# Score differences placed between a tile's two score pairs, half as many of them beside experts, and one list of steps for all units

## What is computed

```python
# attention of layers 0, 1 and 3 (biases and norms left out)
scores = jnp.einsum('bhqd,bhkd->bhqk', q, k) / jnp.sqrt(jnp.float32(8))   # 16 heads, 1024 x 6404
attn = jax.nn.softmax(scores, axis=-1)            # layer 2: jax.nn.sigmoid(scores)
ctx = jnp.einsum('bhqk,bhkd->bhqd', attn, v)
x = x + ctx @ Wo.T
# experts, layer 0 (layers 1 and 3 also gated, layer 1 run twice; layer 2: gelu, not gated)
h = silu(a) * g                                   # a, g = halves of x @ c_fc[e]
x = x + sum over the two chosen experts of weight * (h @ c_proj[e])
```

## Time and profile before

| | |
|---|---|
| median of 3 runs | 4747.94 us (4747.63 to 4750.8) |
| profiled execution, its own time | 4733.75 us |
| its span, first to last instruction | 4731.8 us |
| mean granted TensorE clock | 0.953 |
| busy: PE / DVE / ACT / POOL | 84% / 59% / 84% / 18% |
| busy in us: DVE / ACT | 2803.3 / 3983.6 |

### The profile page before, as it was taken

The page is one execution under the profiler, slowest core; times in us unless marked ns, Lnnn a source line. Parts: engine busy times, 40 slices in busy tenths (PEclk is TensorE's granted clock), DMA queues, the critical chain, the costliest instruction groups (busy, mean ns, idle before and its releaser), DMA issues. The chain is left out here.

```text
span 4731.8 us, 68983 instructions
## 1 busy us (share of the span) xinstructions
PE 3965.9 (84%) x26742; PEld 911.7 (19%) x26742; DVE 2803.3 (59%) x5598; ACT 3983.6 (84%) x4403; POOL 829.8 (18%) x719
## 2 busy tenths in 40 slices
PE   3578888888888888888898999888888888888887
PEld 2112111111112221122112222111111111122112
DVE  1487888778877778877610111011287568886833
ACT  2478998889978898888899888978998888888994
POOL 3001000340014410143522011012001120035002
PEclk7579999999989999999999999999999999999998
DMA  2212000110002110011102121100001100011001
GB/s 73 84 42 56 20 13 18 31 29 10 13 26 56 30 47 10 19 47 35 37 13 61 37 74 40 35 31 26 13 13 36 32 13 13 14 32 32 10 1 47
DMA packets 105922, 150.33 MB, mean 32 GB/s; under 512 B 23064, under 2 KB 64032, under 8 KB 105584
## 3 DMA queue, kind: packets, MB, share of 16 engines
q1 hardware_dynamic: 105584, 145.82, 10.9%
HBM read 122.24 MB, written 23.51 MB: 31 GB/s over the span
## 5 line engine op out<-in xcount | busy, mean ns | idle before, releaser
L913 ACT ACTIVATE prob<-scores 128x1024 f32<-128x1024 f32 x3264 | 3177.3, 1025 | 274.4 <-PE scores L748 259.6
L1022 DVE TENSOR_REDUCE mpart<-side 128x1 f32<-128x512 f32 (+1 forms) x3312 | 2039.4, 656 | 707.8 <-PE side L779 697.5
L758 PE MATMUL av<-prob,VB 128*9 128x512 f32 x6528 | 873.3, 607 | 1.3 <-ACT prob L913 0.5
L758 PE MATMUL av<-prob,VA 128*9 128x512 f32 x6528 | 869.5, 605 | 1.7 <-ACT prob L913 0.8
L748 PE MATMUL scores<-QP,KA 32*128 32x512 f16 x3264 | 640.7, 393 | 195.2 <-ACT above L921 118.2
L748 PE MATMUL scores<-QP,KB 32*128 32x512 f16 x3264 | 630.5, 388 | 195.0 <-ACT above L921 94.2
L779 PE MATMUL side<-KB,QP 32*128 32x512 f16 (+1 forms) x2112 | 583.8, 385 | 43.0 <-DVE mpart L1022 29.1
L779 PE MATMUL side<-KA,QP 32*128 32x512 f16 (+1 forms) x1936 | 534.0, 378 | 33.3 <-DVE mpart L1022 19.4
L1026 DVE CUSTOM_DVE_ANT_0 above<-side,above 128x512 f32<-128x512 f32 x736 | 493.0, 685 | 69.9 <-PE side L779 68.1
L921 ACT ACTIVATE above<-scores 128x1024 f32<-128x1024 f32 x368 | 376.8, 1024 | 169.1 <-PE scores L770 118.1
L748 PEld LDWEIGHTS scores<-QP,KB 32*128 32x128 f16 x3264 | 151.8, 91 | 867.7 <-ACT prob L913 538.6
(11 more groups left out here) (200 smaller groups left out, 2787.3 us busy)
## 6 DMA issues: line engine op xcount, KB each, us to landing
cwb<-weights SPq DMA_DIRECT2D x80, 256.0 KB, 3.8
KA<-kstacks SPq DMA_DIRECT2D x192, 96.0 KB
KB<-kstacks SPq DMA_DIRECT2D x192, 96.0 KB
Fin<-in_Fin SPq DMA_DIRECT2D x64, 256.0 KB, 2.8
kstacks<-hi SPq DMA_DIRECT2D x112, 128.0 KB, 2.4
ctxc<-in_ctxT SPq DMA_DIRECT2D x48, 256.0 KB, 3.0
kstacks<-lo SPq DMA_DIRECT2D x56, 128.0 KB, 2.6
hT<-in_mask SPq DMA_DIRECT2D x16, 400.2 KB, 3.3
```

What stands on the lines that cost most here:

```text
L758: last = pe.matmul(AV[ROWS * h:ROWS * h + VC, :], V[l % 2][:, kt, g * HG + h, :], prob[:, (e + h // 2) % RING, (h % 2) * QB:(h % 2) * QB + ...
L913: act.activation(prob[:, e % RING, :], pair.rearrange("p a b -> p (a b)"), ACT.Exp if softmax(l) else ACT.Sigmoid, scale=SCALE).then_inc(s ...
L1022: dve.tensor_reduce(part, bank, AX.X, ALU.max).then_inc(sem["red"], 1)
```

## The change

1. Where a dif is due it now stands at q = 1, between the two score pairs of a tile, if no background PE step has that slot; av of the tile before follows it at once instead of standing at q = 3. A dif that finds no such slot for 20 slots goes to q = 3, ahead of av and not behind it.
2. `folded(p)` is 2 instead of 4 for eleven phases p (5, 6, 9, 10, 13, 14, 15, 25, 26, 29, 30), whose maxima are found during phases 4, 5, 8, 9, 12, 13, 14, 24, 25, 28 and 29. There only query tiles 0 and 1 are folded: 8 difs and 8 relus instead of 16, 16 DVE instructions on `above` instead of 32, and 176 plain reduces instead of 144.
3. `mpart` gets a column for each chunk; a new DVE step `mclr` (a memset) fills the columns that a folded query tile leaves out, once a phase, and `fina` reads 13 columns instead of 11.
4. Units 0 to 7 and the end of unit 7 are one list inside `nc.If`; the other side has its own copy of units 2 to 7. The barrier and the jump between units 1 and 2 are gone; a jump over the other side now stands at the end.

```diff
-HALVES = [[(qt, c, 2 * half + j) for qt in range(QT) for c in range(2 * NDIF, NCH) for j in range(2)] for half in range(2)]
+HALVES = [[(qt, c, 2 * half + j) for qt in range(QT) for c in range(NCH) for j in range(2)] for half in range(2)]
...
+def folded(p):
+
+    return 2 if p in (5, 6, 9, 10, 13, 14, 15, 25, 26, 29, 30) else QT
+
+
+def singles(p, half):
+
+    return [i for i, (qt, c, h) in enumerate(ITEMS[:FIRST_BOTH]) if h // 2 == half and (c >= 2 * NDIF or qt >= folded(p))]
+
+
+def pairs(p, half):
+
+    return [i for i, (qt, c, h) in enumerate(ITEMS) if i >= FIRST_BOTH and h // 2 == half and qt < folded(p)]
...
+            single, both = [singles(p, half) for half in range(2)], [pairs(p, half) for half in range(2)]
+            spent, ready = 0.0, [[], []]
+            difs = NDIF * 2 * folded(p)
+            ahead = [(a + (e - 24 - a) * d // difs, d) for d in range(difs)]
+            total = len(single[0] + single[1]) * COST["red"] + len(both[0] + both[1]) * COST["both"]
+            out.append(Step("DVE", "mclr", (p,)))
...
+        due = has and ahead and ahead[0][0] <= t and not ready[0] and not ready[1]
+        if due and (q == 1 and kt and t not in taken or q == 3 and t > ahead[0][0] + 20):
+            d = ahead.pop(0)[1]
+            out.append(Step("PE", "dif", (p, d)))
+            out.append(Step("ACT", "relu", (p, d)))
+            ready[DIFS[d][1]].append(t + 7 - q)
+            if q == 1:
+                out.append(Step("PE", "av", (t // Q, kt - 1)))
+                early = True
         if q == 3:
-            if kt:
+            if kt and not early:
                 out.append(Step("PE", "av", (t // Q, kt - 1)))
...
             if has:
                 find(0 if len(single[0] + both[0]) > len(single[1] + both[1]) else 1, t, 1)
-            if has and ahead and ahead[0][0] <= t and not ready[0] and not ready[1]:
-                d = ahead.pop(0)[1]
-                out.append(Step("PE", "dif", (p, d)))
-                out.append(Step("ACT", "relu", (p, d)))
-                ready[DIFS[d][1]].append(t + 5)
...
+                elif s.what == "mclr":
+                    p, = s.key
+                    wait_ge(*o.sem("fina", p - 1))
+                    dve.memset(mpart[:, 0:folded(p), :, 0:2 * NDIF:2], LEAST).then_inc(sem["bgV"], 1)
...
-            run(layer0)
+            run(attention_steps(range(8)) + plain(finish_steps(7)))
         with nc.Else():
+            layer0 = attention_steps([0, 1])
...
-        run(attention_steps(range(2, 8)))
-        run(plain(finish_steps(7)))
+            run(attention_steps(range(2, 8)) + plain(finish_steps(7)))
```

More of the change, by code:

```diff
@@ L92, in both_of @@
     qt, half, i = DIFS[d]
-    return [ITEMS.index((qt, 2 * i + 1, 2 * half + j)) for j in range(2)]
-def column_of(c):
-    return c if c >= 2 * NDIF else NDIF + c // 2
+    return [ITEMS.index((qt, 2 * i + 1, 2 * half + j), FIRST_BOTH) for j in range(2)]
+def folded(p):
[4 more added lines that the diff above has]
+    return [i for i, (qt, c, h) in enumerate(ITEMS) if i >= FIRST_BOTH and h // 2 == half and qt < folded(p)]
 ITEM_DIF = {i: d for d in range(len(DIFS)) for i in both_of(d)}
@@ L461, in attention_steps @@
     p = first + 1
-    spent, single, both, ready, ahead, total = 0.0, [], [], [], [], None
+    spent, single, both, ready, ahead, total, early = 0.0, [], [], [], [], None, False
     def find(half, t, most):
@@ L917, in scalar @@
                     wait_ge(*o.sem("dif", p, d))
-                    for i in both_of(d - 1):
+                    for i in both_of(d - 1 if d else 2 * NDIF * folded(p - 1) - 1):
                         wait_ge(*(o.sem("red", p, i) if d else o.sem("red", p - 1, i)))
@@ L1018, in vector @@
                     wait_ge(*o.sem("max", p, i))
-                    wait_ge(*o.sem("fina", p - 1))
-                    bank, part = bank_of(o, "max", p, i)[:, 0:chunk_of(c)], mpart[:, qt, h, column_of(c):column_of(c) + 1]
+                    wait_ge(*o.sem("mclr", p))
+                    bank, part = bank_of(o, "max", p, i)[:, 0:chunk_of(c)], mpart[:, qt, h, c:c + 1]
                     if i < FIRST_BOTH:
@@ L1026, in vector @@
                         dve.tensor_tensor_reduce(more, bank, more, 1.0, LEAST, ALU.add, ALU.max, part).then_inc(sem["red"], 1)
+                elif s.what == "mclr":
+                    p, = s.key
+                    wait_ge(*o.sem("fina", p - 1))
+                    dve.memset(mpart[:, 0:folded(p), :, 0:2 * NDIF:2], LEAST).then_inc(sem["bgV"], 1)
                 elif s.what == "fina":
-                    for i in (len(HALVES[0]) - 1, FIRST_BOTH - 1, FIRST_BOTH + len(BOTH[0]) - 1, len(ITEMS) - 1):
-                        wait_ge(*o.sem("red", *s.key, i))
-                    dve.tensor_reduce(mm[:], mpart[:, :, :, NDIF:], AX.X, ALU.max).then_inc(sem["bgV"], 1)
+                    p, = s.key
+                    for half in range(2):
+                        wait_ge(*o.sem("red", p, singles(p, half)[-1]))
+                        wait_ge(*o.sem("red", p, pairs(p, half)[-1]))
+                    dve.tensor_reduce(mm[:], mpart[:], AX.X, ALU.max).then_inc(sem["bgV"], 1)
                 elif s.what == "finb":
@@ L1791, in build @@
         barrier()
-        layer0 = attention_steps([0, 1])
-        in_attention = ("score", "exp", "av", "drain", "oT", "rden", "norm", "dif", "relu", "max", "red", "fina", "finb", "finc", "flipmax", "fill", "kload")
+        in_attention = ("score", "exp", "av", "drain", "oT", "rden", "norm", "mclr", "dif", "relu", "max", "red", "fina", "finb", "finc", "flipmax",
+                        "fill", "kload")
         n = nc.values_load(mcount[0:1, 0:1], min_val=0, max_val=P)
         with nc.If(n == P):
-            run(layer0)
+            run(attention_steps(range(8)) + plain(finish_steps(7)))
         with nc.Else():
+            layer0 = attention_steps([0, 1])
             masked_unit(0)
```

3 lines of the change are left out of this document (2 added, 1 removed).

## The result

| | before | after |
|---|---|---|
| median of 19 runs each, us | 4738.15 (4725.36 to 4793.05) | 4720.85 (4699.44 to 4733.6) |
| profiled execution's span, us | 4731.8 | 4718.7 |
| mean granted TensorE clock | 0.953 | 0.944 |
| busy: PE / DVE / ACT | 84% / 59% / 84% | 86% / 61% / 83% |

The ratio after to before is 0.9951, 95% interval [0.9934, 0.9968]: 23 us faster by it, where 148 were forecast. The measured 4720.85 us lie above the forecast's 4600 and its whole range, 4548 to 4700.

What follows compares the result with a forecast made beforehand. The prediction took ACT's work, plus stalls handed on by PE's order, as the bound. Its terms, -60 - 54 - 25 - 13 + 3 + 1 = -148 us, took 4747.94 to 4600 us, range 4548 to 4700.

Steps and rivals of the forecast that it cites:

- (a): Twelve phases with maxima but few or no experts, 193 difs moved to q = 1: -60 us, bounds -89 and 0.
- I take 0.15 for 0.46: ACT idle per dif at q = 1, in us: 0.15 as at an expert's `up`, instead of 0.46 before relus.
- The first rival: Early av delays the second score, so the stall moves to the next exp: -88 us, 4660 us, chance 0.24.
- I count nothing for it: The 52 difs left in phases 5, 9, 13, 14, 25, 29, now ahead of av: 0, up to -24 us.
- (b): Phases 5, 9, 13, 14, 25, 29: 39 relus go, each with its idle, -54 us; -36 if only their own time.
- (c): Phases 4, 8, 12, 24, 28, fewer relus: -25 us, DVE limiting the part without experts; bounds -65 and 0.
- 83%: hidden: Phase 5: DVE gets 7.3 us more, stands at 119 of about 143 us, so its added reduces cost nothing.
- the join: Units 1 and 2 in one list: ACT's idle between them and the low TensorE clock behind it go, -13 us.
- The last rival: Eleven phases beside experts: DVE's added reduces become the bound, +95 us, 4843 us, chance 0.08.
- (d): Between units 1 and 2: idle -7.4 us and low clock behind it -5.7 us, together -13, bounds -7.4 and -13.
- (e): The new jump at the kernel's end: +3 us, bounds 0 and 4.8.
- (f): `mclr`'s 23 memsets and the wider `fina` on DVE: +1 us, bounds 0 and 8.

Runs made afterwards that it cites:

- The fold alone: Kernel before with one list and eight difs in the eleven phases, dif still at q = 3 behind av and a max: ratio 0.9921.
- half reduces: Kernel before with DVE's reduces and its instructions on `above` reading half of their columns: 0.9707, 4603.62 us.
- the pace: Kernel before with one list and 16 difs at q = 3, maxima spent by the sum of ACT's durations, not by slots: 0.9883, 4684.28 us.
- The half-reduce pair: DVE's instructions reading half of their columns in both kernels: kernel before 0.9707, 4603.62 us; changed kernel 0.9437, 4476.83 us.
- the last paced fold: Kernel before with one list, fold, dif at q = 3, maxima paced by ACT's durations, 16 difs again in phases 25 and 26: 0.9821, 4656.75 us.

## Why the prediction was wrong

**(a), -60: failed.** Measured 0 in the whole as the change has it (0.9970 to 0.9969), -21 with av left late; in its own twelve phases -9 and -26. The step that failed is "I take 0.15 for 0.46": the relu's idle did go, to 0.07 us each, but the idle before exps grew, so that "the stall just moves to the next exp, 0" was nearly the true end of the bounds. The `up` matmul was a bad proxy; that its idle was read in phases where DVE had room is the likely reason, not a tested one. The first rival had the mechanism, though the time came out 61 us above its 4660. Its evidence, 1112 waits on DVE, was right in kind, but most of their 841.8 us passed under running matmuls.

**The new place beside experts, counted as nothing: failed.** "I count nothing for it" stands in (b) for the difs that go ahead of av, and (c) has no term for theirs. In the eleven phases the placement cost 18 us without the fold and 42 on top of it. With av left late these are -2 and +24. This and (a) together are why the change as a whole shows so little.

**(b) and (c), -54 and -25: failed in size.** The fold alone brought -24 and -3. The step that failed is the price: a relu less was taken at its full 1.38 us beside experts because DVE stood at "83%: hidden", and it brought 0.6 us in the phases of (b). Mean load is not cover: half reduces and the pace both gave time back at unchanged relus, 134 and 41 us. That DVE is fed in bursts in some tiles and not in others, and that PE's order waits at each burst, is how these runs are best explained; it was not seen tile by tile. PE's own work, 92% of phase 5 with the fold, is a rival that stays open. In the changed kernel both gains were gone: -5 and +9 against before, the second with the join's gain in phase 8 inside it. (c) warned that "DVE takes over", but for phase 4 alone and at no loss. The last rival's sign came true in phases 4, 12, 24 and 28, 8.5, 3.9, 1.3 and 4.1 us longer, yet not by its price, and its other sign did not: DVE was busy only 69.95 of 88.6 us in phase 4's first part, less than before, and PE's weight loads waited 853.2 us for the plain reduces, not over 1000. What rose was PE, with a low clock; no term and no rival had the clock in it outside the join. One bound of (c) was added up too low: at 88% the first part costs 5 us and the last third gives 4, which is +1 for a phase and not 0 in all.

Of the signs named: 280 relus came; their idle fell below the 30 to 60; phase 2 stayed at 123.0 (116 to 120 forecast), phase 5 at 151.3 (141 to 145) with DVE at 79%; phase 4 lost 8.5 us instead of gaining under 8; and idle before exps grew by 211 us where relus lost 149, the sign set for the first rival.

**(d), -13: right or a little small.** 14 us by the ratio of the list alone, its jump included, where (d) and (e) together said 10; phases 7 and 8 lasted 17 us less. The low clock was gone with the list alone; in the changed kernel some of it is back (0.91).

**(e), +3: right in sign.** The last DMA issue of the kernel before, in the timeline:

```profile
4728.91 0.40 SPq L1442 DMA_DIRECT2D out_x<-xs  x1
```

And of the changed kernel:

```profile
4711.85 0.39 SPq L1463 DMA_DIRECT2D out_x<-xs  x1
```

To the span's end it is 2.9 us before (4731.8) and 6.9 after (4718.7): the end got 3.9 us longer, within the 0 to 4.8. The Trainium skill (Runtime: NRT & Kernel Launch, Instruction fetch mechanics) has a taken branch out of the fetched window stall its engine; the 3.9 us agree with that. The list alone ends so too (6.4), and the kernel before with half reduces, without the jump, takes 2.9; no run had the jump without the joined list.

**(f)** is too small for any run here to show.

**The sum.** The list gives 14 us; the placement 0; the fold on top of the placement 0.9969 to 0.9951, 9 us with overlapping intervals. The chance of 0.89 for faster held, by the term that was the surest; that it held is no credit to the two large terms. The range failed because both large terms rested on one assumption, that the path runs through ACT, and were given bounds as if they were independent. The half-reduce pair puts about 105 us on that assumption, some 20 of them by way of the clock.

## What to carry to other kernels

An engine can be the busiest, here at 84%, and still not repay work taken off it, while an in-order engine feeds it and waits in turn for a third. Before pricing such work, ask what the feeding engine waits for, here a ring of three banks emptied by an engine at 59%. Halve that third engine's work in an experiment first: if the gain appears only then, spread or cut its work instead, as pacing did here for 41 us. A moved stall is only worth what the instruction behind it had in slack, and idle before both must be added up. A wait that passes under running work costs nothing: read the engine's own idle time beside it. And add up a reordering over all the phases that it touches, those priced at nothing too.

## What was not expected of the hardware

- The granted clock moved with the order of PE's instructions at nearly equal work. The medians of all runs are 0.954 for the list alone, 0.9475 with 16 difs in each phase and the new place for them and av, 0.944 for the changed kernel, 0.882 with av ahead of the maxima. The kernel before has 0.950, and its runs lie between 0.945 and 0.956.
- It moves between kernels even where nothing was changed. Phase 20 has the same 689 matmuls before and in the last paced fold, and lasted 128.0 and 134.2 us in the one trace of each. The kernel before:

```profile
3011.80:3139.80 128.00, 114.27 (x689) 25.93 (x690) 16.99 (x47) 110.21 (x114) 14.15 (x10) 0.96 0.13 39
```

And the paced fold with 16 difs again in two phases:

```profile
2942.40:3076.60 134.20, 120.56 (x689) 26.46 (x690) 17.01 (x47) 110.43 (x115) 14.16 (x10) 0.91 0.12 37
```

So a difference of some 5 to 10 us between the traces of two kernels can be such luck, and the smaller differences between phases above are not shown to be more than that.
